# Attention that projects two tiles ahead and turns K and Q by a trip through memory and VectorE

## The reference

```python
q, k, v = x @ Wq, x @ Wk, x @ Wv                    # 512 -> 16 heads x 128
q, k = rmsnorm(q, q_rms_w), rmsnorm(k, k_rms_w)     # over the 128 of a head
scores = q k^T / sqrt(128) - slope[head] * (t - s)  # causal
y = rmsnorm(softmax(scores) @ v, subln_w)
x = layernorm(x + y @ Wproj)
x = layernorm(x + mixture(x))                       # 8 experts, top 2, squared relu
```

## Time and profile before

| | |
|---|---|
| runs | 1438.0, 1438.51, 1438.63 us, median 1438.51 |
| the profiled execution | 1442.51 us, its span 1440.7 us |
| granted TensorE clock, mean | 0.992 |
| busy in the span | PE 97%, DVE 56%, ACT 51%, POOL 29% |
| attention | from the start to 960.4 us; 1076 us: last token routed |
| steps of one iteration start at | 429.41 (i = 0), 441.54, 454.85, 470.14; next iteration 487.58 |
| the first step | 21.1 to 34.5 us |
| the last steps (60 to 63) start at | 894.6, 909.6, 922.9, 938.7; end 960.4 |
| step 63, head 2 (no projection beside it) | scores from 947.41, probabilities turned from 950.10 |
| a subtraction on VectorE, 128x512, first operand x_raw / kt_ps | 682 ns / 685 ns |
| two block transposes, one behind the other (L533) | 1.30 us |

### The profile page before, as it was taken

How to read it: one execution, slowest core, us unless ns; L and a number is a source line. 1 busy time by engine, 2 the same in 40 slices (tenths; PEclk the granted TensorE clock), 3 DMA queues, 4 the chain that set the end, 5 groups by cost and what they waited for, 6 DMA issues and landing times. The chain is left out here.

```text
span 1440.7 us, 26432 instructions
## 1 busy us (share of the span) xinstructions
PE 1400.9 (97%) x7744; PEld 1184.6 (82%) x7745; DVE 813.3 (56%) x1877; ACT 730.3 (51%) x1633; POOL 424.2 (29%) x410
## 2 busy tenths in 40 slices
PE   8999999999999999999999999999999989999994
PEld 6888888888888888888888888878887868888783
DVE  6555655656556555555565555567777763333334
ACT  5565656656556566566565565543333223333334
POOL 1212221212112122222121212103445553353565
PEclk9999999999999999999999999999999999999997
DMA  5243333232433333333334245557659546756699
GB/s 185 75 130 95 109 95 115 88 113 91 131 95 109 95 96 108 96 107 109 117 89 115 76 128 157 143 136 171 148 137 233 176 139 247 265 201 230 187 192 237
DMA packets 136851, 200.45 MB, mean 139 GB/s; under 512 B 16624, under 2 KB 83312, under 8 KB 133488
## 3 DMA queue, kind: packets, MB, share of 16 engines
q1 hardware_dynamic: 126032, 149.67, 36.0%
q0 software_dynamic: 10784, 50.36, 11.9%
HBM read 160.05 MB, written 92.62 MB: 175 GB/s over the span
## 5 line engine op out<-in xcount | busy, mean ns | idle before, releaser
L413 POOL TENSOR_TENSOR small<-small,half 128x4 f32<-128x4 f32 x193 | 195.0, 1010 | 764.2 <-DVE small L443 764.2
L557 DVE CUSTOM_DVE_ANT_0 logit<-score_ps,bias 128x128 f32<-128x128 f32 (+3 forms) x256 | 124.8, 487 | 157.1 <-PE score_ps L699 117.6
L347 ACT ACTIVATE prob<-logit,small 128x128 f32<-128x128 f32 (+3 forms) x256 | 144.2, 563 | 120.1 <-DVE small L557 116.5
L712 PEld LDWEIGHTS y_ps<-vs,prob_t 128*128 128x128 f32 x1280 | 175.1, 191 | 21.5 <-ACT prob_t L354 4.5
L712 PE MATMUL y_ps<-vs,prob_t 128*128 (+1 forms) x1280 | 185.6, 276 | 0.7 <-ACT prob_t L354 0.7
L354 ACT ACTIVATE prob_t<-prob_ps 128x128 f32<-128x128 f32 (+3 forms) x256 | 111.5, 436 | 54.9 <-PE prob_ps L705 53.9
L705 PE MATMUL prob_ps<-ident,prob 128*128 128x128 f32 x640 | 112.8, 274 | 3.2 <-ACT prob L347 2.8
L443 DVE TENSOR_REDUCE small<-squares 128x4 f32<-128x516 f32 x128 | 88.4, 691 | 45.7 <-ACT squares L269 43.8
L631 PE MATMUL v_ps<-w_hi,x_hi 128*128 (+1 forms) x256 | 106.7, 417 | 1.4 <-DVE w_lo L488 1.4
L929 ACT ACTIVATE yt_hi<-x_raw,subln 128x512 fp32r<-128x512 f32 x60 | 43.2, 723 | 126.2 <-DVE x_raw L1025 51.2
L631 PE MATMUL v_ps<-w_hi,x_lo 128*128 (+1 forms) x256 | 106.6, 416 | 0.0
(11 more groups left out here) (233 smaller groups left out, 3370.0 us busy)
## 6 DMA issues: line engine op xcount, KB each, us to landing
slots_x<-in_zeros SPq DMA_DIRECT2D x64, 512.0 KB, 4.4
y_scratch<-x_now SPq DMA_DIRECT2D x65, 256.0 KB, 2.8
x_raw<-in_x_t SPq DMA_DIRECT2D x64, 256.0 KB, 2.6
slots_y<-in_zeros SPq DMA_DIRECT2D x64, 256.0 KB, 4.4
y_raw<-y_scratch SPq DMA_DIRECT2D x56, 256.0 KB
w_raw<-in_w_experts POOLq DMA_DIRECT2D x7, 2048.0 KB
w_hi<-in_w_experts POOLq DMA_DIRECT2D x7, 2048.0 KB
w_raw<-in_w_all SPq DMA_DIRECT2D x16, 768.0 KB, 6.1
```

Source lines behind the costliest of these rows:

```text
L347: nc.scalar.activation(prob[:, 0:width], logit[:, 0:width], ACT.Exp, scale=-1.0, bias=least[:, h:h + 1], accum_out=row_sum[:, (i % 2) * HG ...
L413: nc.gpsimd.tensor_tensor(r, ms, half[:, :], ALU.pow).then_inc(ready, 1)
L557: nc.vector.tensor_tensor_reduce(out=logit[:, 0:width], in0=score_ps[:, 0:width], in1=bias[:, h, T - width:T], scale=1.0, scalar=3e38, op0 ...
L712: mm = nc.tensor.matmul(y_ps[:, :].rearrange("p (b h i) -> p h b i", b=QB, h=HG)[:, h, :, :], prob_t[:, j * P:(j + 1) * P], one(vs[:, bass ...
```

## The change

K and Q of a tile are normalised one step earlier than before, stored to memory by SP, loaded back as 32-row blocks in the next step, and turned there by VectorE's block transpose. For that the projections run two tiles ahead. Its core:

```diff
@@ sync @@
+            def store_kq(t):
+                sp.wait_ge(k_normed, t + 1)
+                sp.wait_ge(q_normed, t + 1)
...
+                    sp.wait_ge(kq_loaded, (t - 1) * (16 * QB))
+                sp.dma_start(kq_scratch, kq[:, :]).then_inc(kq_stored, 16)
+            def load_kq(t):
+                sp.wait_ge(kq_stored, t * 16)
...
+                sp.wait_ge(k_turned, t)
+                sp.wait_ge(q_turned, t)
+                rows = kq_scratch.rearrange("(a j) (b c) -> b j a c", a=QB, b=QB)
+                for b in range(QB):
+                    sp.dma_start(kq_in[b * QP:(b + 1) * QP, :].rearrange("p (a c) -> p a c", a=QB), rows[b])\
+                        .then_inc(kq_loaded, 16)
+            store_kq(1)
                 for i in range(TB):
...
+                        load_kq(it * TB + i + 1)
...
+                    if not (last and i >= TB - 2):
+                        store_kq(it * TB + i + 2)
@@ scalar @@
-                    if i < 3:
+                    for m in ((0,), (1, 2), (), ())[i]:
                         act.wait_ge(w_loaded, it * 16 + 16)
...
-                        round_k(nxt, nxt_i, n + 2)
+                        round_k(nxt, nxt_i, n + 2, kt)
...
-                    if ahead:
-                        round_q(nxt_i, n + 2)
+                    if i > 0 and ahead:
+                        round_q(nxt_i, n + 2, qt)
...
                     keep_prob_t(3)
+                    if i == 0:
+                        round_q(nxt_i, n + 2, qt)
@@ vector @@
+            def normalise_part(m, src, r, ready, count, done):
+                dve.wait_ge(ready, count)
...
+                    dve.wait_ge(kq_stored, (count - 2) * 16)
+                nc.vector.tensor_tensor(kq_parts[:, m], src[:, :].rearrange("p (h b i) -> p h b i", h=HG, b=QB),
+                                        r.unsqueeze(2).unsqueeze(3).to_broadcast([P, HG, QB, QP]), ALU.mult)\
+                    .then_inc(done, 1)
+            def turn_part(m, out, t, ready, done):
+                dve.wait_ge(kq_loaded, t * (16 * QB))
+                dve.wait_ge(ready, t)
+                nc.vector.transpose(turned_columns(out), in_parts[:, m]).then_inc(done, 1)
...
                     logits(2)
                     if ahead:
-                        normalise(qn[:, :], q_ps, q_r, q_rstd, n + 2, q_normed)
+                        turn_part(1, kt, n + 1, k_ready, k_turned)
+                    if i > 0 and ahead:
+                        turn_part(0, qt, n + 1, q_ready, q_turned)
+                    if projects:
+                        normalise_part(0, q_ps, q_r, q_rstd, n + 3, q_normed)
...
                     logits(3)
+                    if i == 0:
+                        turn_part(0, qt, n + 1, q_ready, q_turned)
@@ tensor @@
+            pe.wait_ge(x_ready, 2)
+            project(k_ps, 1, 1, 0).then_inc(k_projected, 1)
+            project(q_ps, 0, 1, 0).then_inc(q_projected, 1)
+            pe.wait_ge(v_ready, 1)
+            project(v_ps, 2, 1, 0).then_inc(v_projected, 1)
...
-                        turn(kt_ps, kn, k_turned)
...
-                        turn(qt_ps, qn[:, :], q_turned)
```

More of the change, by code:

```diff
@@ L342, in body @@
                     nxt, nxt_i = (it % 2, i + 1) if i < TB - 1 else ((it + 1) % 2, 0)
+                    far, far_i = (it % 2, i + 2) if i < TB - 2 else ((it + 1) % 2, i + 2 - TB)
                     ahead = not (last and i == TB - 1)
+                    projects = not (last and i >= TB - 2)
                     def softmax(h):
@@ L424, in body @@
                     rstd_y(it * TB + i + 1)
-                    if not (last and i == TB - 1):
-                        rstd_kq(it * TB + i + 2)
+                    if not (last and i >= TB - 2):
+                        rstd_kq(it * TB + i + 3)
             nc.gpsimd.memset(logit[:, 0:P], 0.0).then_inc(fill_set, 1)
@@ L430, in _ @@
             rstd_kq(1)
+            rstd_kq(2)
             with pool.Fori(0, last_it) as it:
@@ L552, in body, with split_w @@
                     ahead = not (last and i == TB - 1)
+                    projects = not (last and i >= TB - 2)
+                    def split_w(m):
+                        dve.wait_ge(w_rounded, it * 3 + 3 * CT + m + 1)
+                        blk = w_block((hg + 1) % 2, m, b)
+                        nc.vector.tensor_tensor(
+                            one(w_lo[:, bass.ds(blk, 1), :]), one(w_raw[:, bass.ds(raw_block(it, m), 1), :]),
+                            one(w_hi[:, bass.ds(blk, 1), :]), ALU.subtract).then_inc(w_ready, 1)
                     def logits(h):
@@ L568, in body @@
                     logits(1)
-                    if ahead:
-                        normalise(kn[:, :], k_ps, k_r, k_rstd, n + 2, k_normed)
-                    if last and i == TB - 2:
+                    if projects:
+                        normalise_part(1, k_ps, k_r, k_rstd, n + 3, k_normed)
+                    if not ahead:
+                        dve.wait_ge(early_loaded, 16 + 32 * QB)
+                        turn_y(3)
+                    if not (last and i >= 1):
+                        split_x((i + 1) % 2, n + 4)
@@ L572, in body @@
+                    if projects:
+                        row_means(kq_sq, q_ms, q_squared, n + 3, q_summed)
+                    if last and i == TB - 3:
                         dve.wait_ge(early_loaded, 16 + 16 * QB)
                         turn_y(0)
-                    if not ahead:
+                    if last and i == TB - 2:
                         turn_y(2)
-                        turn_y(3)
-                    if not (last and i >= 2):
-                        split_x(i % 2, n + 3)
@@ L586, in body @@
+                    if not ahead:
                         split_y(3)
-                    if last and i == TB - 2:
+                    if last and i == TB - 3:
                         turn_y(1)
                     logits(3)
-                    if last and i == TB - 2:
+                    if i == 0:
+                        turn_part(0, qt, n + 1, q_ready, q_turned)
+                    if last and i == TB - 3:
                         split_y(0)
                         split_y(1)
+                    if last and i == TB - 2:
+                        split_y(2)
@@ L682, in body @@
                     now = it % 2
-                    xb = (i + 1) % 2
-                    wp = (it // B) % 2 if i < TB - 1 else ((it + 1) // B) % 2
+                    xb = i % 2
+                    wp = (it // B) % 2 if i < TB - 2 else ((it + 1) // B) % 2
                     width = P * (i + 1)
                     ahead = not (last and i == TB - 1)
+                    projects = not (last and i >= TB - 2)
                     def score(h):
```

241 lines of the change are left out of this document (130 added, 111 removed).

## The result

The changed kernel takes 1449.61 us (median of 4 runs, 1447.62 to 1451.34) against 1438.57 before in the same comparison: the ratio is 1.0065, with a 95% interval of 1.0048 to 1.0082. It is slower by 7 to 12 us where 18 us less was forecast; the range ended at 1438.

The account below looks back on a forecast made before the run. TensorE was taken to bound attention, busy 856.62 of 860.10 us. +7.6 (front) - 24 (loop) + 2.5 (step 60) - 4 (end) = -18 us from the 1438.51 us median gave 1420.5 us, range 1398 to 1438.

Parts of the forecast that it names:

- An iteration thus gains -0.15 + 0.2 + 0.7 + 0.75 = 1.5 us; I take 1.6: Attention loop: gains of steps i = 0 to 3 of an iteration; over fifteen iterations 24 us.
- The price of the slots: TensorE in the loop: eight identity products removed are worth 0.86 us a step, 54 us in all, if no wait remains.
- the base: Whole kernel before: median of 1438.51 us taken as start, the profiled run being 4.0 us over it.
- score(0) of the next step 441.7: End of step i = 0: next score starts at 441.7 against 441.54, behind Q's late rounding and split; a loss of 0.15 us.
- at nothing: Loop's other operations, same with another source or layout: cost nothing; ScalarE's two roundings may cost 0.05 us more each.
- gain 0.75: Step i = 3, the wider one: longer covers, so it gains 0.75 us.
- the trip hidden: K and Q stored to memory and loaded back: hidden at i = 0 to 1, margin 1.5 us; high end costs 1.4.
- Step 60, +2.4 for +2.5: Near attention's end: K and Q load behind the clearing lands 4.5 us late and holds VectorE; +2.5 us (0 to 6).
- the tie at i = 2: Step i = 2: VectorE's line with two turns ends at 466.25, when score(3) is ready too; could go the wrong way.
- nothing gained: Rival: VectorE's extra work and ScalarE's rounding give back the rest; iteration gains 0.4, ends cost 6: 1438 us, chance 0.1.
- The rival that ends slower (1459): Trip 4 us longer stops VectorE's queue 2.5 us at i = 1: +21 us, 1459; chance 0.12.
- +7.6 + 2.5 - 4 = +6.1 us: Ends of attention: front with second tile's products ahead +7.6, step 60 +2.5, last steps together -4 us.

Follow-up runs that it names:

- experiment 5: Kernel before with K's four identity products made twice: 1464.70 us, iteration 59.59; with six of eight left out: 1406.67 us, iteration 56.01, attention's result changed.
- the pad and all edits: Changed kernel with weights' split earlier, Q's order at i = 0, mended ends, four more order edits and 544 unused bytes: 1415.57 us, ratio to before 0.9826.
- experiment 6: Changed kernel with each of VectorE's two turns cut to 32 of 512 columns: 1448.07 us, iteration 57.66, attention's result changed.
- experiment 2: Changed kernel with Q at i = 0 turned into PSUM in the order of the other steps: ratio to before 1.0006, iteration 57.12 us.
- experiment 7: Unused tiles: changed kernel plus 544 bytes, ratio to before 1.0029; before plus 32 bytes, 1.0018; version with all order edits plus 64 bytes, 1419.81 us.
- experiment 3: Changed kernel with the K and Q store and loads cut to one row each: 1455.03 us, ratio to before 1.0086, attention's result changed.
- experiment 4: Changed kernel with the 2304 KB clearing moved into step 61 and y's two turns behind the last row sums and normalising: ratio to before 0.9989.

## Why the prediction was wrong

**The step that failed** is "An iteration thus gains -0.15 + 0.2 + 0.7 + 0.75 = 1.5 us; I take 1.6". It gained 0.49. The price of the slots, from which it began, was right (experiment 5), and so was the base. The missing 1.1 us are in four places, beside 0.1 that "I take 1.6" put on top of the sum:
- "score(0) of the next step 441.7", -0.15 at i = 0: it was -0.58. Turned as in the other steps, i = 0 is 0.50 us shorter. The text did have the chain over head 3's copy, Q's rounding and split, but laid it with hand-overs near zero; the trace has 0.24 us from the split's end to TensorE's product and the turn of head 3 at 10.43 us into the step, not 10.3.
- The weights' split at the end of i = 1, new in that place for K of i = 2. The text called what stands around the turns "at nothing" and never asked who needs this block and when: 0.18 us.
- The rate of the products: "The other operations are the same". 36 products a step start 3 to 4 ns later each, since other tiles moved by 544 bytes: 0.25 us an iteration, and some in the next phase, where "nothing changes except memory borrowed under other names".
- What is left is some 0.2 us. Most of it is the "gain 0.75" of i = 3, which was not laid out: with the pad and all edits it is 0.58. The chain of softmax ends last there after six of the eight products are gone (experiment 5), so the full 0.86 of a step was not to be had. At i = 2 head 3 is turned 0.68 us earlier in that version, as laid out; the step is 0.61 shorter, and what takes the 0.07 behind it is open.

**Right in mechanism.** i = 1 "hardly shorter" (-0.22 for -0.2, with head 2 turned 0.04 us later and head 3 0.29 earlier, where 0.15 and 0.24 were laid out); the trip hidden, with the low end of its cost; steps 62 and 63 within 0.6 us.

**Right by luck.** Step 60, +2.4 for +2.5. The text let the late K and Q load hold VectorE and through it TensorE. VectorE was held, for 5.1 us, but TensorE waited for the weights. They were issued 5.8 us ahead of step 60 in before and 3.2 ahead in after, where the store of K and Q stands in front of them in SP's queue, and took 14.9 and 14.2 us to land, so they came some 2 us later into the step; TensorE's wait grew from 1.87 to 4.13 us.

**Without weight.** VectorE's turns cost nothing in the loop (experiment 6), and so the tie at i = 2 that the rival "nothing gained" used decided nothing. The rival that ends slower (1459) had the sign, by a mechanism that did not occur: the trip was not late in the loop, and what cost the time were the order of instructions and the place of tiles.

**The ends.** They were put at +7.6 + 2.5 - 4 = +6.1 us and came to +9.95 + 2.4 + 2.0 - 1.2 - 3.4 + 3.4 = +13.2. The start of score(0) varies by run (21.1 to 23.1 us in four profiles of before and its variants, 29.1 to 31.6 in twelve of after and its variants), so 1 to 2 us of the first term are not the change's. The first step was to lose some of its waits and grew by 0.7 us; it has the order of i = 0, and without that order it takes 13.65 us (experiment 2), so 0.5 of the 0.7 are that. Step 61 took 1 us more than the text gave for the turns of y; why was not found. The seam was left out: the last step's queue ends with the second tile's load, which is issued at 953.05 us, behind 17 transfers of that step, and VectorE waits for it ahead of the last row sums.

**The sum**, then: -24 became -6.1 over the fifteen iterations, +6.1 became +13.2 (+12.4 without what the first step grew, which is in both), which is the 6.3 us of the profiles. The medians differ by 11. Before's profiled run was 4 us above its median and after's 2 us below its own; where in the run those lie was not found, so some 6 us of the measured difference have no place in this account.

On the Trainium skill's rule that spoke against the change ("VectorE: DVE Perf Modes", section "Rules for kernel authors": a 128x128 transpose to TensorE where PSUM will do): here no transpose by VectorE was on the path, and its 693 ns against 193 made no difference, while eight on TensorE cost some 0.8 us a step. In this kernel, which TensorE bounds, the measurements go against the rule. What they don't give is the change's full worth with the same repairs on both sides.

## What to carry to other kernels

When work leaves the engine that bounds a kernel, price the removal, and then follow each moved instruction to whoever reads its result: here two lines of order (Q's rounding behind a copy, a weight split behind Q's), one bulk transfer ahead of urgent ones and one wait at the seam undid a change that with these mended is 0.7% under before. When two transfers are late, look at which of them the bounding engine waits for: here the wait that was forecast was there, on VectorE, and another one counted. A wait shorter than a product's modelled end is not in the waits of a profile; compare start to start. And compare the rate of an instruction that has not changed: if it differs, look at where its operands lie.

## What the runs showed of the hardware

- **Addresses.** In an unbroken run a 128x512 fp32r product starts every 229.2 or 233.3 ns by the SBUF address of tiles: moving x_hi, x_lo and all behind them by 32 or 544 bytes switches it, 64 bytes change nothing (experiment 7).
- **The queue.** 768 KB of weights issued right behind 2304 KB of clearing landed 14.2 to 15.0 us after their issue in three profiles (before, after and experiment 3), and 5.3 us after it where the clearing was moved behind them (experiment 4).
- **The clock.** In step 60 a wait of 4.13 us was followed by 3.4 us at the lower clock, and without the wait the clock stayed at 1.00.
- **Slots.** Four more 128x128 identity products cost 0.39 to 0.43 us a step where TensorE did not wait, 0.19 where it did (experiment 5).
